# Second shared expert: batch 1's up products and all of batch 0's down products ahead of the route, its weights' second copy ahead of the routed rows

## The reference

```python
x = x + attention_a(layernorm(x))      # 16 heads of 128, causal
x = x + ffn(layernorm(x))
x = x + attention_b(layernorm(x))      # low-rank q and kv, rotary part
x = x + ffn(layernorm(x))              # the same weights again

def ffn(x):                            # 2048 tokens, D 512, 8 experts of hidden size 256
    logits = xf @ gate_w
    top_logits, top_idx = top_k(logits, 2)
    gates = softmax(top_logits) on the two chosen experts, else 0
    h = gelu(xf @ w1[e] + b1[e]);  out_e = h @ w2[e] + b2[e]
    routed = sum over e of gates[e] * out_e
    shared = gelu(xf @ shared_w1 + shared_b1) @ shared_w2 + shared_b2   # hidden size 512
    return routed + shared
```

## Time and profile before

| | us |
|---|---|
| median of 3 runs | 2440.26 |
| lowest, highest | 2439.38, 2440.95 |
| profiled execution, its own time | 2442.46 |
| span of the profiled execution | 2440.7 |
| TensorE busy in the span | 2306.0 (94%) |
| VectorE busy | 1661.4 (68%) |
| ScalarE busy | 1120.8 (46%) |
| GpSimd busy | 611.0 (25%) |
| route of layer 0, first product of tile 0 to last of tile 38 | 1167.2 to 1319.1 |
| route of layer 1, the same | 2242.2 to 2394.9 |

### The profile page before, as it was taken

One profiled execution on the slowest core, in us unless ns is written; L12 is line 12 of the kernel. 1 busy time (PEld: TensorE's weight loads), 2 busy tenths in 40 slices (PEclk: granted clock), 3 DMA queues, 4 the chain that ended last, 5 costly groups with the idle time before them and its releaser, 6 DMA issues. The chain is left out here.

```text
span 2440.7 us, 40753 instructions
## 1 busy us (share of the span) xinstructions
PE 2306.0 (94%) x12966; PEld 1979.7 (81%) x12966; DVE 1661.4 (68%) x3852; ACT 1120.8 (46%) x2649; POOL 611.0 (25%) x497
## 2 busy tenths in 40 slices
PE   6999999999999999978999779999999999889997
PEld 5889898989898988856788558888888888767886
DVE  7555555564655554577666748998998999975666
ACT  3444444343434443443333435665666566542334
POOL 1111111110111111135121323333333333234223
PEclk9999999999999999989999889999999999999998
DMA  4524333334242424224885200000000000017866
GB/s 167 180 93 141 132 109 136 132 104 168 92 179 92 154 104 143 105 86 184 295 284 189 77 19 1 19 19 0 18 18 18 0 18 18 18 53 272 278 237 233
DMA packets 101006, 279.83 MB, mean 115 GB/s; under 512 B 8840, under 2 KB 11272, under 8 KB 95264
## 3 DMA queue, kind: packets, MB, share of 16 engines
q1 hardware_dynamic: 80032, 222.81, 25.9%
q0 software_dynamic: 11360, 37.76, 4.0%
q10 hardware_dynamic: 9504, 17.85, 2.2%
HBM read 133.40 MB, written 144.98 MB: 114 GB/s over the span
## 5 line engine op out<-in xcount | busy, mean ns | idle before, releaser
L74 PE MATMUL bank<-xT_hi,w_hi 128*128 128x512 f32 x864 | 349.7, 405 | 18.6 <-POOL w_lo L700 5.7
L76 PE MATMUL bank<-xT_hi,w_lo 128*128 128x512 f32 x864 | 343.3, 397 | 0.0
L75 PE MATMUL bank<-xT_lo,w_hi 128*128 128x512 f32 x864 | 343.3, 397 | 0.0
L619 DVE TENSOR_TENSOR hq_lo<-bank,hq_hi 128x512 fp32r<-128x512 f32 (+1 forms) x256 | 157.1, 624 | 251.5 <-ACT hq_hi L555 104.7
L609 DVE SCALAR_TENSOR_TENSOR x<-bank,inv,x 128x512 f32<-128x512 f32 x256 | 182.0, 748 | 170.6 <-PE bank L76 170.6
L74 PE MATMUL bank<-wo_hi,hq_hi 128*128 128x512 f32 x576 | 232.3, 403 | 15.3 <-DVE x L1050 13.7
L75 PE MATMUL bank<-wo_lo,hq_hi 128*128 128x512 f32 x576 | 226.7, 393 | 0.0
L76 PE MATMUL bank<-wo_hi,hq_lo 128*128 128x512 f32 x576 | 226.5, 393 | 0.0
L74 PEld LDWEIGHTS bank<-xT_hi,w_hi 128*128 128x128 f32 x864 | 166.2, 192 | 54.8 <-DVE xT_lo L178 9.8
L76 PEld LDWEIGHTS bank<-xT_hi,w_lo 128*128 128x128 f32 x864 | 165.5, 192 | 35.6
L75 PEld LDWEIGHTS bank<-xT_lo,w_hi 128*128 128x128 f32 x864 | 165.8, 192 | 33.9
(11 more groups left out here) (297 smaller groups left out, 6309.4 us busy)
## 6 DMA issues: line engine op xcount, KB each, us to landing
sorted_x<-blank SPq DMA_DIRECT2D x48, 1584.0 KB, 10.9
arena<-split_w SPq DMA_DIRECT2D x32, 1024.0 KB, 5.9
split_w<-arena SPq DMA_DIRECT2D x48, 512.0 KB, 3.0
raw<-dram_wr SPq DMA_DIRECT2D x24, 512.0 KB, 5.9
w_raw<-dram_wa SPq DMA_DIRECT2D x16, 512.0 KB, 3.8
arrived<-routed_y SPq DMA_DIRECT2D x8, 1024.0 KB, 8.2
w_raw<-dram_wb SPq DMA_DIRECT2D x8, 768.0 KB, 4.4
row_pt_hi<-sorted_x ACTq DMA_DIRECT2D x22, 264.0 KB, 4.2
```

What stands on the lines that cost most here:

```text
L74: nc.tensor.matmul(out, hi, mov_hi, start=first, stop=False)
L75: nc.tensor.matmul(out, hi, mov_lo, start=False, stop=False)
L76: return nc.tensor.matmul(out, lo, mov_hi, start=False, stop=last)
L619: return nc.vector.tensor_tensor(out, bank, hi.bitcast(F32), ALU.subtract).then_inc(done, 1)
```

## The change

TensorE's list: `down(B)` now stands whole ahead of the two turns; both `up(B + 1, ...)` stand behind them, ahead of the route. Behind the route the first up is that of B + 2. The wait in `input_for` is for one shared step more. ScalarE's and VectorE's steps of B + 1 move with it, VectorE waits for its own rests of B + 1 ahead of the route (the buffer `hid` is also the route's), and the wait for the last tile's turn goes from B + 1 to B + 2 on ScalarE. SyncE loads the second copy of the second half's up weights right behind expert 0, ahead of its wait for the scatters, and waits for the up products of v = 3 first, which read `w`.

```diff
@@ -1598,7 +1598,7 @@
         pe.wait_ge(rt.xs_lo, i0 + i + 1)
         ge(pe, rt.biased, i0 + i - 1)
         if i < 2:
-            pe.wait_ge(f.gelu_done, KH * (s0 + B + 1))
+            pe.wait_ge(f.gelu_done, KH * (s0 + B + 2))
 
     def slot_for(expert):
 
@@ -1692,9 +1692,11 @@
     up(B, 0, 0)
     up(B, 0, 1)
     down(3, (0, 1, 2, 3))
+    down(B, (0, 1, 2, 3))
     turn(0)
     turn(1)
-    down(B, (0, 1))
+    up(B + 1, 1, 0)
+    up(B + 1, 1, 1)
 
     pe.wait_ge(rt.tables_out, TABLES_OUT * (L + 1))
     input_for(0)
@@ -1706,18 +1708,14 @@
         if i:
             expert = route_down(i - 1, before, i + 1 < TILES)
         else:
-            down(B, (2, 3))
             expert = expert_of(1)
             input_for(1)
         if i + 1 < TILES:
             coming = slot_for(expert)
         turn_hidden(i)
         before, slot = slot, coming
-    up(B + 1, 1, 0)
+    up(B + 2, 2, 0)
     route_down(TILES - 1, before)
-    up(B + 1, 1, 1)
-
-    up(B + 2, 2, 0)
     up(B + 2, 2, 1)
     pe.wait_ge(rt.y_out, i0 + TILES)
     down(B + 1, (0, 1, 2, 3))
@@ -1740,7 +1738,7 @@
         s, slot = s0 + v, HQ_SLOT[v]
         act.wait_ge(f.up_done, KH * s + j + 1)
         ge(act, f.h_lo, KH * s - KH + j + 1)
-        if v == B + 1 and j == 0:
+        if v == B + 2 and j == 0:
             act.wait_ge(rt.h_turned, i0 + TILES)
         nc.scalar.activation(m.hid[:, j, :], m.bank[j][:, :], ACT.Gelu,
                              bias=m.b1[:, v // B, j:j + 1]).then_inc(f.gelu_done, 1)
@@ -1823,6 +1821,8 @@
     input_hi(0)
     input_hi(1)
     load(RING)
+    hidden(B + 1, 0)
+    hidden(B + 1, 1)
     for i in range(TILES):
         gelu(i)
         if i + 2 < TILES:
@@ -1834,7 +1834,7 @@
             nc.scalar.activation(m.gap_exp[:, :], m.gap[:, :], ACT.Exp).then_inc(g.exp_done, 1)
         hidden_hi(i)
 
-    for v in range(B + 1, 2 * B):
+    for v in range(B + 2, 2 * B):
         hidden(v, 0)
         hidden(v, 1)
     root(0)
@@ -1939,12 +1939,15 @@
     rest(B, 0)
     rest(B, 1)
     add(3)
+    add(B)
     dve.wait_ge(rt.tables_out, TABLES_OUT * (L + 1))
     input_lo(0)
     mark(0)
     input_lo(1)
     mark(1)
-    add(B, (0, 1))
+    rest(B + 1, 0)
+    rest(B + 1, 1)
+    dve.wait_ge(f.h_lo, KH * (s0 + B + 2))
     before = None
     for i in range(TILES):
         expert = dve.value_load(m.tab[0:1, E_AT + i:E_AT + i + 1], min_val=0, max_val=E - 1)
@@ -1954,19 +1957,15 @@
             mark(i + 2)
         if i:
             output(i - 1, before)
-        else:
-            add(B, (2, 3))
         if i == 3:
             gate_vector(nc, dve, m, g, L)
         hidden_lo(i)
         before = expert
     output(TILES - 1, before)
 
-    rest(B + 1, 0)
-    rest(B + 1, 1)
+    add(B + 1)
     rest(B + 2, 0)
     rest(B + 2, 1)
-    add(B + 1)
     combine_vector(nc, dve, m, rt, L, 0)
     rest(B + 3, 0)
     rest(B + 3, 1)
@@ -2128,6 +2127,8 @@
         sp.wait_ge(rt.w_ready, 64 * E)
     sp.wait_ge(rt.scattered[0], 32 * GT * (L + 1))
     load_slot(0)
+    sp.wait_ge(f.up_done, KH * (s0 + B))
+    load_split(sp, ws, 2 * E + 2, whole, [t[:, 0:1024] for t in m.w], f.w1_in)
     sp.wait_ge(rt.tables_out, TABLES_OUT * (L + 1))
     sp.wait_ge(rt.scattered[1], 32 * GT * (L + 1))
     for i in range(RING):
@@ -2137,7 +2138,6 @@
         load_rows(sp, m, rt, xs_d, i, block)
     sp.wait_ge(rt.w_ready, 64 * (E * L + 1))
     load_slot(1)
-    load_split(sp, ws, 2 * E + 2, whole, [t[:, 0:1024] for t in m.w], f.w1_in)
     sp.wait_ge(f.y_done, NT * (s0 + B))
     between()
     for e in range(2, E):
```

## The result

The changed kernel takes 2448.21 us (median of 7 runs, 2445.28 to 2449.86) against 2440.26 us for the kernel before in the same call: a ratio of **1.0031**, 95% interval 1.0021 to 1.0041, so 5 to 10 us slower. The forecast was 2440.8 us, too little to tell from no change, with a range up to 2447.0: the kernel is measurably slower and its time lies 1.2 us outside the range. The profiled execution of the changed kernel took 2447.22 us with a span of 2445.4; against the earlier trace rows's execution (2442.46 and 2440.7) that is only +4.7 us, since the one lies 1.0 us under its median and the other 2.2 us over its own. So the trace can explain 4.7 us step by step, and the ratio says that some 3 us more are usual.

A forecast was written before the change was run, and what follows sets the result against it. TensorE, busy 94% of the span, was taken as the bound, with a hole ahead of each route. Terms 5.6 - 1.5 - 3.6 = +0.5 us, added to the median 2440.26, gave 2440.8 us, range 2436 to 2447.

The forecast's parts named there:

- What bounds the kernel, and that the hole can be filled: Ahead of each route: TensorE idles 5.69 us, then runs slowly, about 8.5 us a layer; 5.44 us of down products fill it.
- it would have been 3 us earlier: Tile 1's first product, had the down products filled the hole and nothing taken its place.
- What d is: How much later the last scatter ahead of the route lands beside the early copy: 1.4 us, bounds 0 and 5.6.
- d = 3.0: Last scatter's delay if it took the 5.8 us of a load's middle; the sum would be +3.7 us.
- The read and what follows 1.2, Gelu 0.69, tile 0's own chain: Ahead of tile 1: Gelu wait 0.69 us, number read 1.2, then tile 0's uncovered 2.70; tile 1 1.4 us + d later.
- the rival that happened: Clock falls in the 1.9 and 1.0 us gaps behind the up products: 1.7 us a layer, 2444.2 us; chance 0.20.
- Layer 0's end, -1.5 us: Behind layer 0's route: the combination of batch 0 waits for its rows, so all moves 2.0 us earlier, less 0.5 for clock.
- The 0.5 us for the clock behind the longer wait: Layer 0's end: TensorE's wait for VectorE grows from 2.87 to about 6.3 us, with 0.5 us charged for slower clock.
- Layer 1's end, -3.6 us: Behind layer 1's route: rows land at 2406.9, gathering follows at 2416.5 instead of 2420.1; kernel's end moves by -3.6 us.
- ScalarE's 5.09 us wait: ScalarE's copy of batch 2's first hidden half waits for the last routed rows; hidden by 10.9 us of TensorE work.
- starts +5.6: Start of the route in both layers: 2 x (1.4 + 1.4) = 5.6 us lost.
- ends -5.1: Behind the routes: -1.5 us in layer 0 and -3.6 us in layer 1.

The follow-up runs named there:

- e2_down_only: The kernel before with all 24 down products of batch 0 ahead of the turns, up products and copy at their old places; 2434.11 us, ratio 0.9969.
- e1_copy_only: The kernel before with SyncE's early second copy alone, no product moved; 2446.26 us, ratio 1.0011.
- e7_no_copy: The changed kernel with the second copy left out, so batches 1 to 3 of the second half use the first half's up weights; 2443.79 us, ratio 1.0003.
- e10_half_copy: The kernel before with only the `w_hi` half (512 KB) of the second copy loaded early, `w_lo` at its old place; 2443.33 us, ratio 1.0002.
- e11_down_filler: The kernel before with batch 0's down products ahead of the turns and unread filler products in the four gaps behind them; 2433.09 us, ratio 0.9964.
- e8_filler: The changed kernel with nine products whose results nobody reads ahead of the first turn; 2446.84 us, ratio 1.0019.
- e3_read_ahead: The changed kernel with the expert's number of tile 0 read behind the turns, ahead of the moved up products; 2448.41 us, ratio 1.0026.
- e6_down_read: The kernel before with batch 0's down products, and the read of tile 0's expert number, ahead of the turns; 2434.97 us, ratio 0.9966.

## Why the prediction was wrong

**What bounds the kernel, and that the hole can be filled:** right. The hole of 5.69 us and the slow stretch behind it, 8.5 us a layer in the prediction, are there; e2_down_only collects 8 us from both layers together. The prediction gave this part alone one sentence ("it would have been 3 us earlier"; e2_down_only has 2.4 and 4.7) and no sum of its own, and so never asked whether the rest of the change pays for itself.

**"What d is", 1.4 us in each layer: the first step that failed.** It is 2.8 us in layer 0 and 2.1 in layer 1 (last scatter 5.6 and 4.9 us). The prediction took the landing time of a scatter for something that the load does to it at the moment of its issue, and read 4.0 us, 0.4 us before the load's end, as the value near the end. It is the length of a backlog: the earlier trace rows's 5.8, 4.0 and 2.8 are its draining, and with the copy behind the first load the backlog stays at 7.3 to 7.5 us for three or four scatters more and drains from there. This gives 4.0 in e1_copy_only's layer 0 and, without the jump, would give 4.2 in the changed kernel's: the value that the prediction took, by luck, from another mechanism. The other 1.4 us of layer 0 and 1.0 us of layer 1 (4.9 where the row was falling to 3.9) are the jump, a term that the prediction had at nothing. In layer 0 it came with the moved down products and not with the copy: e7_no_copy has it too (d = 1.1 us without a copy), e1_copy_only has not. It stands beside the instruction packet each time; that this is the cause stays open.

The rule that the prediction cited from the Trainium skill, "DMA: Bandwidth & Descriptors", section on queues, rings and completion order, is that an engine takes turns between the queues that have work, packet by packet. The trace agrees in so far as the scatters keep landing beside the pending loads, from 1145.6 to 1153.4 in the changed kernel. The estimate that stood beside it in the prediction, d = 3.0, was nearer than my 1.4.

**"The read and what follows 1.2, Gelu 0.69, tile 0's own chain": right.** The gap ahead of the route is 2.00 and 1.81 us for 1.9, the hidden tile's 0.36 (at the low clock) and 0.78 for 1.0, and e7_no_copy's layer 1 gives 1.48 us for 1.4 + d with no d.

**The clock: the rival that happened, with a larger price.** The forecast left it out, the rival had it behind the up products at 1.7 us a layer. In layer 0 it fell at the first turn, behind the 3.04 us that the larger d had opened: from tile 1's turn to tile 1's first product it is 14.02 us where the prediction's working gives 10.75, so 3.3 us, of which a second fall at 1176.6, behind the 2.00 us gap, is a part; 1.2 us more went in the first tiles. In layer 1, with gaps of 2.00, 0.93, 1.81 and 0.78 us, it held: 11.06 us for 10.75. The +7.44 us of layer 0 is 1.4 + 2.8 + 3.2, the +3.71 of layer 1 is 1.4 + 2.1 + 0.2. The prediction wrote that this rival "with a d over 1.9" leaves the bound; d was 2.8 and 2.1. Its range ended at 2447.0 with 1.7 us a layer for the fall and d = 2.8 in both; layer 0 alone lost 4.4 to it. With the measured starts and ends in place of the predicted ones (+12.6 and -4.3, below) the prediction's own sum gives 2448.6 us, beside the median of 2448.21.

**Layer 0's end, -1.5 us: half right.** The combination did come to wait for its rows, but its start moved by 1.2 us against the last output, not by 2.0: the second load, issued at 1331.7, took 8.3 us to land, where the earlier trace rows had 7.5. The 0.5 us for the clock behind the longer wait (7.08 us, 6.3 forecast) measured 0.47. Together -0.75.

**Layer 1's end, -3.6 us: right,** measured -3.5, though by other numbers on the way, so in part by luck: the combination is 2.7 us nearer to the last output, the first gathering 2.9, the rest comes as sums and gatherings disturb each other less (the first gathering takes 4.69 us; in the trace of before it took 6.08). The prediction put the second load's issue at 2400.0; in the trace of before it is 2399.7, a slip of 0.3 us. ScalarE's 5.09 us wait was free, as said.

**The sum.** Forecast: starts +5.6, ends -5.1. In the trace: starts 7.44 + 3.71 + 1.23 + 0.25 = +12.6, ends -4.3, entry -0.8, attention -2.8, together +4.7. The starts were undervalued by 7 us: 2.1 by d, about 4.7 by the clock.

## What to carry to other kernels

When an edit has two halves that can be made apart (here the down products that fill a hole, and a load brought forward so that more can be moved), cost them apart: the one may pay for the other. Before a load is put beside a stream of small indirect DMAs that something waits for, follow the landing time of each of them: if it is several times the issue interval there is a backlog, and what counts is whether enough of them are left behind the load's end for it to drain. And when work is moved into a hole whose end a DMA sets, ask what clock the engine will have behind the gaps that remain: in layer 0 the falls behind gaps of 3.0 and 2.0 us cost 4.4 us, where the hole that was filled had been 5.7 us long.

## What the runs showed of the hardware

- Scatters issued 1.27 us apart land 0.70 us apart once the loads beside them have ended; during the loads each takes 7 to 8.7 us, alone 2.7 to 2.8. So 1 MB issued 15 us ahead of the last scatter, and landed within 0.3 us of its issue, still made that scatter land later, in layer 0 by 1.2 us (e1_copy_only against before) or 1.8 (the changed kernel against e7_no_copy).
- A 16 KB instruction packet stands beside each case in which a scatter's landing time jumps or halts late in the draining row (layer 0: 2.9 to 3.9 us in e7_no_copy, 4.8 to 5.6 in the changed kernel), and where it is missing or comes 16 us before the last scatter, the row falls evenly (before, e1_copy_only and e10_half_copy in layer 0, e11_down_filler in layer 1). Moving 24 products ahead moved the packet from 12.6 us behind the last scatter to within 2.3 us of it. No run shows that the one causes the other.
- TensorE's granted clock fell from 2.4 to 1.2 GHz at gaps of about 1 us: in e2_down_only's layer 0 it was 1.00 in the turn behind a gap of 0.95 us and fell to 0.50 within the turn behind the next gap, 0.91 us, which began 0.7 us later. In layer 1 of the same run, with gaps of 0.85 and 1.09 us, it held, and e8_filler's layer 1 lost it with gaps (0.82, 1.79) that e7_no_copy's layer 1 (0.86, 1.78) got through. The length of single gaps does not foretell it here.
- Reading the register earlier took 0.8 to 1.0 us out of the gap ahead of the route (e3_read_ahead), and tile 1 came 0.8 and 0.4 us earlier in e6_down_read; neither median shows a gain.
